# A cross attention step with wider sum products, and a tile's queries, weights and projection at other places

## The reference, cut to what matters

```
q = h @ Wq                                  # h: normalized x, INNER = 16 * 64
out_txt = softmax(q @ (ctx[:77] @ Wk).T / 8)    @ (ctx[:77] @ Wv)
out_img = softmax(q @ (ctx[77:] @ Wk_ip).T / 8) @ (ctx[77:] @ Wv_ip)
x = x + (out_txt + out_img) @ Wo + bo
```

## Time and profile before

| | |
|---|---|
| median of three runs | 2460.3 us |
| the profiled execution's own time | 2435.73 us |
| its span, first to last instruction | 2433.6 us |
| PE busy in the span | 2160.2 us, 89% |
| DVE, ACT, POOL busy | 65%, 38%, 36% |
| products L2271 (the sums) | 4608, of 256 columns |
| steps in the stage | 128, from 624 to 2034 us |

### The profile page before, as it was taken

One profiled execution on the slowest core, in us unless ns is written; L12 is line 12 of the kernel. 1 busy time (PEld: TensorE's weight loads), 2 busy tenths in 40 slices (PEclk: granted clock), 3 DMA queues, 4 the chain that ended last, 5 costly groups with the idle time before them and its releaser, 6 DMA issues. The chain is left out here.

```text
span 2433.6 us, 37422 instructions
## 1 busy us (share of the span) xinstructions
PE 2160.2 (89%) x13637; PEld 1726.1 (71%) x13637; DVE 1570.4 (65%) x2756; ACT 925.0 (38%) x1869; POOL 877.5 (36%) x535
## 2 busy tenths in 40 slices
PE   5878877796699999999999999999999997787897
PEld 3445545464598889888898998998998994334684
DVE  4179934333577677677677677777776763795554
ACT  1166611210244344344344444444443443452331
POOL 1066412431343333243343333343333300362455
PEclk8989977798899999999999999999999998798898
DMA  5800002511476677677676777776776656001364
GB/s 159 169 16 14 8 1 88 230 50 57 145 200 184 185 218 205 185 217 206 185 217 180 226 202 208 198 207 199 202 211 186 194 156 248 4 0 44 98 148 114
DMA packets 229957, 362.99 MB, mean 149 GB/s; under 512 B 41920, under 2 KB 197824, under 8 KB 225168
## 3 DMA queue, kind: packets, MB, share of 16 engines
q1 hardware_dynamic: 223008, 342.08, 48.1%
q0 software_dynamic: 6768, 18.49, 3.2%
HBM read 234.97 MB, written 125.50 MB: 148 GB/s over the span
## 5 line engine op out<-in xcount | busy, mean ns | idle before, releaser
L2271 PE MATMUL img_ps<-cn,pt_hi 128*128 128x256 f32 (+1 forms) x3072 | 569.7, 287 | 3.0 <-DVE pt_lo L2478 3.0
L2271 PEld LDWEIGHTS img_ps<-cn,pt_hi 128*128 128x128 f32 (+1 forms) x3072 | 477.3, 191 | 3.2 <-issue 3.2
L2271 PE MATMUL img_ps<-cn,pt_lo 128*128 128x256 f32 (+1 forms) x1536 | 435.9, 284 | 0.0
L2466 DVE STREAM_TRANSPOSE prob_blocks<-prob 128x384 f32<-128x384 f32 x512 | 250.6, 547 | 183.8 <-ACT prob L2402 175.9
L2248 PE MATMUL s_ps<-ct,a_hi 128*128 128x508 f32 x768 | 315.7, 411 | 0.0
L2249 PE MATMUL s_ps<-ct,a_hi 128*128 128x508 f32 x768 | 304.2, 396 | 0.0
L2250 PE MATMUL s_ps<-ct,a_lo 128*128 128x508 f32 x768 | 304.0, 396 | 0.0
L2001 POOL TENSOR_SCALAR ct<-staged 128x762 fp32r<-128x762 f32 x64 | 136.8, 2138 | 439.6 <-DMA staged<-in_ctx_t 312.5
L2271 PEld LDWEIGHTS img_ps<-cn,pt_lo 128*128 128x128 f32 (+1 forms) x1536 | 292.6, 190 | 0.0
L2478 DVE TENSOR_TENSOR pt_lo<-prob_moved,pt_hi 128x768 fp32r<-128x768 f32 x256 | 277.9, 1124 | 9.4 <-ACT pt_hi L2414 9.2
L2001 POOL TENSOR_SCALAR cn<-staged 128x768 fp32r<-128x768 f32 x64 | 137.4, 2147 | 376.5 <-DMA staged<-in_ctx_n 293.4
(11 more groups left out here) (370 smaller groups left out, 3712.9 us busy)
## 6 DMA issues: line engine op xcount, KB each, us to landing
prob_rows<-prob_blocks SPq DMA_DIRECT2D x512, 192.0 KB, 2.1
prob_moved<-prob_rows SPq DMA_DIRECT2D x512, 192.0 KB, 3.6
staged<-in_ctx_n SPq DMA_DIRECT2D x64, 384.0 KB, 4.7
staged<-in_ctx_t SPq DMA_DIRECT2D x64, 381.0 KB, 4.7
up_all_m<-in_up SPq DMA_DIRECT2D x8, 2048.0 KB, 12.8
down_all_m<-in_down SPq DMA_DIRECT2D x8, 1024.0 KB, 23.4
sums_m<-y_b SPq DMA_DIRECT2D x63, 128.0 KB, 2.2
w_shared<-in_wq SPq DMA_DIRECT2D x7, 1024.0 KB, 7.3
```

Source lines behind the costliest of these rows:

```text
L2271: last = nc.tensor.matmul(img_ps[:, 0:D], left[0:n, j, :], rows[0:n, right, j, :], start=j == 0 and at == 0, stop=j == IB - 1 and at == 2)
L2466: nc.vector.transpose(blocks[:, m], source[:, m]).then_inc(turned, 1)
```

## The change

It does five things.

1. A tile's queries are made between the text scores and the image scores of the last step, and their copies stand first in ACT's and DVE's lists of that step. `key_side(g+1)` and the copies of `a` then stand where they stand in every other step.
2. The sums: the high part of the probabilities is multiplied with high and low rows in one product of 512 columns, and the low part with the high rows in one of 256, added to the second half of the bank. 36 products in a step become 24.
3. Both halves of the bank are added and scaled: ACT scales the second half into `o` (new), and DVE's operation becomes a scale and add of the first half and `o`.
4. The projection is made one step later (the tile's fourth), before `value_side` of that step; the loops get one more round for the last tile.
5. `wo` and `wq` are loaded in two halves of 512 KB, in the steps with n = 0 and 1, and n = 6 and 7.

```
@@ -2102,7 +2103,7 @@
 
         def projects(g):
 
-            return g // STEPS - 1 if g % STEPS == 2 and g >= STEPS else None
+            return g // STEPS - 1 if g % STEPS == 3 and g >= STEPS else None
 
         def half(h):
             return slice(h * IB // 2, (h + 1) * IB // 2)
@@ -2156,14 +2157,16 @@
                 if n == 0 and i:
                     sp.wait_ge(scored, g)
                     load_keys(i, 1)
+                if n < 2 and i:
+                    heads = slice(n * PAIRS1 // 2, (n + 1) * PAIRS1 // 2)
                     sp.wait_ge(queried, i + 1)
-                    sp.dma_start(wo, src["wo1"]).then_inc(wo_in, 16)
+                    sp.dma_start(wo[:, heads], src["wo1"][:, heads]).then_inc(wo_in, 16)
                 if n == 4 and i:
                     sp.wait_ge(v_used, 2 * i)
                     load_values(i, 1)
-                if n == 5 and 1 <= i < NT - 1:
+                if n in (6, 7) and 1 <= i < NT - 1:
                     sp.wait_ge(projected, i)
-                    sp.dma_start(wq, src["wq1"]).then_inc(wq_in, 16)
+                    sp.dma_start(wq[:, n - 6], src["wq1"][:, n - 6]).then_inc(wq_in, 16)
                 if n == 12 and i < NT - 1:
                     sp.wait_ge(scored, i * STEPS + 12)
                     load_keys(i + 1, 0)
@@ -2267,9 +2270,9 @@
                     pe.wait_ge(split_done, 2 * g + h + 1)
                     for j in range(IB)[half(h)]:
                         n = min(P, IMG - j * P)
-                        for at, (left, right) in enumerate(((pt_hi, 0), (pt_hi, 1), (pt_lo, 0))):
-                            last = nc.tensor.matmul(img_ps[:, 0:D], left[0:n, j, :], rows[0:n, right, j, :],
-                                                    start=j == 0 and at == 0, stop=j == IB - 1 and at == 2)
+                        nc.tensor.matmul(img_ps[:], pt_hi[0:n, j, :], rows[0:n, :, j, :], start=j == 0, stop=False)
+                        last = nc.tensor.matmul(img_ps[:, D:2 * D], pt_lo[0:n, j, :], rows[0:n, 0, j, :],
+                                                start=False, stop=j == IB - 1)
                     last.then_inc(summed if h else half_summed, 1)
 
             def turn_sums(g):
@@ -2296,10 +2299,9 @@
                                             start=False, stop=True)
                 last.then_inc(t_done[bank], 1)
 
-            def project(t):
-                kept(ring.place(1))
-                if t < NT - 1:
-                    pe.wait_ge(wo_in, 16 * (t + 1))
+            def project(t, head_place):
+                kept(head_place)
+                pe.wait_ge(wo_in, 32 * min(t + 1, NT - 1))
                 for side in range(2):
                     bank = use()
                     cols = slice(side * P, (side + 1) * P)
@@ -2314,36 +2316,36 @@
             for place in q_places:
                 kept(place)
             a_place = key_side(0)
-            for g in range(N + 3):
+            for g in range(N + 4):
                 if g < N:
                     if g:
                         pe.wait_ge(exp_done, g)
                     kept(a_place)
                     text_scores(g)
+                    if boundary(g):
+                        if g > STEPS:
+                            pe.wait_ge(wq_in, 32 * (g // STEPS) + 16)
+                        q_places = queries(g // STEPS + 1)
                     scores(g)
                 if 1 <= g <= N:
                     turn_text(g - 1)
-                if g >= 3:
+                if 3 <= g < N + 3:
                     ot_place = turn_sums(g - 3)
-                if boundary(g):
-                    if g > STEPS:
-                        pe.wait_ge(wq_in, 16 * (g // STEPS) + 16)
-                    q_places = queries(g // STEPS + 1)
-                elif g < N - 1:
+                if g < N - 1:
+                    if boundary(g):
+                        for place in q_places:
+                            kept(place)
                     a_place = key_side(g + 1)
                 if 2 <= g <= N + 1:
                     sums(g - 2)
-                if boundary(g):
-                    for place in q_places:
-                        kept(place)
-                    a_place = key_side(g + 1)
-                if g >= 3:
+                if projects(g) is not None:
+                    project(projects(g), head_place)
+                if 3 <= g < N + 3:
                     if g == 3:
                         pe.wait_ge(wv_in, 16)
                     kept(ot_place)
                     value_side(g - 3)
-                if projects(g) is not None:
-                    project(projects(g))
+                    head_place = ring.place(1)
 
         def keep(eng, copy, ring, out, rows=P, cols=BANK):
 
@@ -2388,12 +2390,14 @@
             act.wait_ge(q_zeroed, 1)
             keep_queries(act, copy, 0, ring)
             keep_a(0)
-            for g in range(N + 3):
+            for g in range(N + 4):
+                if boundary(g):
+                    keep_queries(act, copy, 0, ring)
                 if 1 <= g <= N:
                     keep(act, copy, ring, pt_txt[(g - 1) % 3][0:TXT, :], TXT, P)
-                if g >= 3:
+                if 3 <= g < N + 3:
                     keep(act, copy, ring, flat(ot), P, D)
-                if not boundary(g) and g < N - 1:
+                if g < N - 1:
                     keep_a(g + 1)
                 if g < N:
                     act.wait_ge(bias_done, g + 1)
@@ -2404,8 +2408,6 @@
                                          accum_out=total[g % 3][:, 1:2]).then_inc(image_exp, 1)
                     nc.scalar.activation(prob[:, 0:TXT], s_ps[:, 0, 0:TXT], ACT.Exp, bias=bias[g % 2][:, 0:1],
                                          scale=SCALE, accum_out=total[g % 3][:, 0:1]).then_inc(exp_done, 1)
-                if boundary(g):
-                    keep_queries(act, copy, 0, ring)
                 if 1 <= g <= N:
                     act.wait_ge(moved_in[(g - 1) % 2], 16 * Q * ((g - 1) // 2 + 1))
                     for h in range(2):
@@ -2413,16 +2415,21 @@
                             act.wait_ge(summed if h else half_summed, g - 1)
                         nc.scalar.activation(in_quarters(pt_hi, h), by_block(moved[(g - 1) % 2], h),
                                              ACT.Copy).then_inc(pt_hi_kept, 1)
-                if boundary(g):
-                    keep_a(g + 1)
-                if g >= 3:
+                if 2 <= g <= N + 1:
+                    act.wait_ge(summed, g - 1)
+                    act.wait_ge(inv_done, g - 1)
+                    if g >= 3:
+                        act.wait_ge(sums_kept, g - 2)
+                    nc.scalar.activation(o[:], img_ps[:, D:2 * D], ACT.Copy,
+                                         scale=inv[(g - 2) % 3][:, 1:2]).then_inc(part_kept, 1)
+                if projects(g) is not None:
+                    ring.next()
+                    ring.next()
+                if 3 <= g < N + 3:
                     _, b, p, _ = parts(g - 3)
                     keep(act, copy, ring, head_out[:, p, b * S:(b + 1) * S], P, S)
                     if p == PAIRS1 - 1:
                         act.sem_inc(v_used, 1)
-                if projects(g) is not None:
-                    ring.next()
-                    ring.next()
 
         @block.vector
         def _(dve):
@@ -2443,7 +2450,10 @@
             dve.sem_inc(queried, 1)
             keep_a_lo(0)
             dve.wait_ge(pad_zeroed, 1)
-            for g in range(N + 3):
+            for g in range(N + 4):
+                if boundary(g):
+                    keep_queries(dve, copy, 1, ring)
+                    dve.sem_inc(queried, 1)
                 if g < N:
                     dve.wait_ge(scored, g + 1)
                     nc.vector.tensor_reduce(top[g % 2][:, 0:1], s_ps[:, 0, 0:TXT], AX, ALU.max)
@@ -2469,24 +2479,17 @@
                     dve.wait_ge(inv_done, g + 1)
                     nc.vector.tensor_scalar(prob[:, 0:TXT], prob[:, 0:TXT], inv[g % 3][:, 0:1], None,
                                             ALU.mult).then_inc(txt_normed, 1)
-                if boundary(g):
-                    keep_queries(dve, copy, 1, ring)
-                    dve.sem_inc(queried, 1)
                 if 1 <= g <= N:
                     for h in range(2):
                         dve.wait_ge(pt_hi_kept, 2 * (g - 1) + h + 1)
                         nc.vector.tensor_tensor(in_quarters(pt_lo, h), by_block(moved[(g - 1) % 2], h),
                                                 in_quarters(pt_hi, h).bitcast(F32), ALU.subtract).then_inc(split_done, 1)
                 if 2 <= g <= N + 1:
-                    dve.wait_ge(summed, g - 1)
-                    nc.vector.tensor_scalar(o[:], img_ps[:, 0:D], inv[(g - 2) % 3][:, 1:2], None,
-                                            ALU.mult).then_inc(sums_kept, 1)
-                if boundary(g):
-                    keep_a_lo(g + 1)
-                if g >= 3:
```

(6 more changed lines are left out.)

105 lines of the change are left out of this document (55 added, 50 removed).

## The result

The changed kernel took 2418.9 us, the median of four runs (2415.65 to 2420.78), against 2460.6 us of the kernel before beside it: a ratio of 0.9833 (95%: 0.9816 to 0.985), 41.7 us less. The forecast was 2423 us.

The account below looks back on a forecast made before the run. TensorE's list was taken as the bound. Savings 13.7 + 16.0 + 5.5 + 4.5, less 1.8 and 0.5, make 37.4 us: 2435.7 to 2398.3 profiled, 2423 us as median from 2460.3, range 2405 to 2442.

Parts of the forecast that it names:

- What bounds the kernel: Mid-stage TensorE is busy without a gap, so an edit counts by work or waits it takes from TensorE's list.
- Wide sums: In the probability sums, a block of products goes from 0.360 to 0.351 us, 1536 times: 13.7 us saved.
- Boundary: At seven tile boundaries, TensorE's waits and refilling of the array go with the moved queries: 16.0 us saved.
- Clock: Behind three of seven tile boundaries the granted clock fell; without the standing there, 5.5 us saved, between 0 and 6.6.
- Projection: Ahead of the projection, seven of eight waits for `head_out` go, with refilling: 4.5 us saved, between 3 and 5.
- Late `o`: In steps where GpSimd delays VectorE, `o` comes late for its transposes: 1.8 us lost, plus 0.5 in the tail.
- Weights in halves: The half loads of wo and wq stay hidden as before: zero, with 1 us to either side.
- From the profiled execution to the median: Timed runs lie 24.6 us above the profiled one; the same difference was added to 2398.3, giving 2422.9 us.
- (a): Rival in the sums: a 512-column product costs twice a 256-column one, 0.240 us, no gain there; 2437 us, chance 0.15.
- (b): Rival at the boundary: the wait returns at the queries' products or VectorE's copy; 2444 us, chance 0.08.
- (c): Rival at VectorE's `o`: with two inputs, GpSimd holds it up, about 1 us each in 18; 2441 us, chance 0.07.
- (d): Rival in the sums: the wide product is fed slower than the 508-column one, making the kernel slower; chance 0.04.

Follow-up runs that it names:

- first trace of before: The original profiled execution of the unchanged kernel: 2435.7 us, against 2460.3 us for the median of its timed runs.
- the boundary alone: The kernel before with only a tile's queries moved between its last text and image scores, their copies first: 2436.1 us, ratio 0.9924.
- before again: The unchanged kernel, profiled and timed once more for a second trace: median 2455.2 us, ratio 0.9999, profiled at 2454.9 us.

## Why the prediction was right

The time, 2418.9, lies 4 us below the forecast, in a range of 2405 to 2442. Step by step, against the first trace of before:

- **What bounds the kernel.** Right for the boundaries and the projections, whose steps fell by what left the list. Of the 77 ns that left the sums, 47 left the step.
- **Wide sums, 13.7 us.** The mechanism held and the size was off. The step that failed is the reading of the pace: "nine groups of three 256-column products" in one step gave 0.360 us a block, and the mean of the regular steps is 0.358. The pair afterwards is 0.350, as forecast at 0.351. The twelve blocks and their edges give 77 ns a step, 128 x 0.077 = 9.9 us, and the scores give 1.6 of that back, which I had not foreseen. A page had spoken against the edit: by the Trainium skill, "TensorE: Matmul & The Clock Gate", section on the back-to-back issue gap, and the formula that it has there for a single product, the saving would be an estimate of 3.8 us. The measured 9.9 in the sums and about 6 net lie between that and mine. Its pace of 109 ns for 256 columns was seen in no step here: these products take 119 to 120 in the mean, and no two of them start less than 112 ns apart.
- **Boundary, 16.0 us.** 16.0 in the first pair of traces, some 0.4 of it the sums' own gain; the boundary alone has 15.8 against the first trace of before and 17.7 against "before again". The 0.4 us left for something else that is late was hardly needed (0.16 in one step): 13.61 is 10.04 and 3.54 and 0.03.
- **Clock, 5.5 us.** The steps behind the boundaries fell by 76.7 - 70.2 = 6.5 us, of which 0.5 belongs to the sums, so 6.0. The boundary alone does the same, which shows that the standing brought it about and not the other edits. Standing is not enough by itself, though: three or four of seven boundaries before had a fall and the others none.
- **Projection, 4.5 us.** 4.7 alone, against the first trace of before. That "TensorE didn't wait for them during the full loads either" held in that trace and not in "before again", where late probabilities cost a projecting step 1.3 us of wait and 1.6 of clock. In the change it also keeps ScalarE's new copy off the path, without which these steps take 172.9 - 171.4 = 1.5 us more than before, the sums' own gain in them included: a meeting of two edits that I missed.
- **Late `o`, 1.8 us lost.** 17 ns a step, 2.1 us. It is late only in kernels with the wide product: 10 to 15 of 77 regular steps exceed the median by over 0.05 us there, and at most one does in those without. ScalarE's copy takes 0.457 us and not the 0.383 of its twin, which mattered at the projection alone. The tail lost 0.4 us of 0.5.
- **Weights in halves, zero.** No effect that stands out of the spread of the first steps, some 2 us. It was not tried alone.
- **The sum.** 37.4 forecast, 32.4 found; nearly all of the difference is in the wide sums.
- **From the profiled execution to the median.** "More time at the lower clock would do it" was a guess and, by the one further trace, mostly wrong. 13.5 of 19 us lay behind the stage, in a block that the change does not touch. Subtracting the sum from the median was still the right use of it. That the timed gain, 41.7 us, exceeds the stage's 32.4 fits "before again", whose stage is 4.6 us longer, with four clock falls behind boundaries and one at a projection; 37.0 us lie between it and the change. The other 4.7 are within the timed runs' own interval, 36.9 to 45.3 us. So that the time came within 4 us of the forecast is luck in part: the wide sums were put over 5 us too high, and what the timed kernel before loses beyond the first trace, in its stage, was not in the sum.

Of the rivals, (a) is false in its form: 512 columns take 0.23 us and not 0.240. (b) is false: no wait came back at the queries or their copies, and all seven boundaries together gave back 0.16 us in this trace, up to 0.9 in the others. (c) is false: none of the `o` exceeded 0.484 us, seven of them wholly inside a GpSimd operation. The Trainium skill, "SBUF — State Buffer", on the shared port pair, names two SBUF inputs as what contends; the trace agrees, with `pt_lo` stretched to 2.61 us and `o`, one input from PSUM, at 0.48 just behind and never longer. (d) is false: a block is 0.350 and not above 0.375.

## What to carry to other kernels

Read a pace as a mean over all steps before it is multiplied by 1536: one step was 0.7% off, and that was a quarter of the term. An engine that stands at a seam costs more than its wait: seven boundaries gave 16 us and another 6 through the clock behind them, more than the 6 us that 128 steps of the inner loop gave. When an operation is put into an engine's list, look for what stands behind it there in the rare steps as well as in the common one.

## What the runs showed that I had not expected

- The clock fell behind boundaries with at most 2.7 us of standing at a time, in one to four of seven cases, and once at a projecting step, behind a wait of 1.88 us. Behind one of 2.22 us in another kernel it did not fall. In nine traces with the new boundary no step behind one was late.
- Score products come 0.7 ns later in the mean (229.5 to 230.2 ns) when the products of another phase are wide, with the same operands and columns. Only the first nine of 18 do.
- The same program ended its last block in 46.8 us or in 59.5, with VectorE standing on "issue" for over 11 us at a time in the longer case, while GpSimd's gathers kept their 1.25 us.
- One GpSimd addition of 4.57 us cost TensorE 5.6 us: 3.8 of wait, since VectorE's `pt_lo`, two inputs in SBUF, stood as long as it ran, and 1.7 through the clock behind the wait. Eight additions of 0.74 us cost it about 1.4.
- VectorE's scalings, which read one tensor in SBUF, are held up too. That of `prob` (L2480, 128x77) takes 0.26 us at the least and up to 1.95 in the changed kernel; in 82 of 123 steps it takes over 0.3, and 81 of these end 0.05 to 0.07 us behind a GpSimd operation.
